# Cross attention: four places instead of three for the high and low halves of the probabilities

## The reference, cut to what matters

```
qh = (q @ wq.T)  -> 16 heads of 64          q = layernorm(x)
kh = (k @ wk.T), vh = (v @ wv.T)            k = v = ctx_1024
scores = einsum('bhqd,bhkd->bhqk', qh, kh) / sqrt(64)
attn   = softmax(scores, axis=-1)
ctx    = einsum('bhqk,bhkd->bhqd', attn, vh)
x      = x + ctx @ wo.T
```

## Time and profile before

| what | value |
|---|---|
| median of three runs | 3653.69 us |
| lowest, highest | 3648.0, 3655.38 us |
| span of the profiled execution | 3648.2 us |
| busy: TensorE, VectorE, ScalarE, GpSimd | 85%, 74%, 65%, 29% |
| mean granted TensorE clock | 0.937 |
| cross attention, about | 1853 to 3440 us |

### The profile page before, as it was taken

One profiled execution on the slowest core, in us unless ns is written; L12 is line 12 of the kernel. 1 busy time (PEld: TensorE's weight loads), 2 busy tenths in 40 slices (PEclk: granted clock), 3 DMA queues, 4 the chain that ended last, 5 costly groups with the idle time before them and its releaser, 6 DMA issues. The chain is left out here.

```text
span 3648.2 us, 78625 instructions
## 1 busy us (share of the span) xinstructions
PE 3088.9 (85%) x31124; PEld 1836.6 (50%) x31124; DVE 2698.1 (74%) x4017; ACT 2360.0 (65%) x4397; POOL 1058.4 (29%) x1854
## 2 busy tenths in 40 slices
PE   6999999978999755899778888998899879998824
PEld 3747474645665543444345554555455545555411
DVE  4748483867897765444469988889888988889688
ACT  3838373766786534333368887778777887788534
POOL 2232323156446234233212222222222222222122
PEclk9999999989999977999999999999999999999956
DMA  4050505175365376344399999999999999999843
GB/s 151 28 146 29 172 5 146 37 249 149 122 201 165 94 251 208 81 119 127 92 220 190 190 199 199 199 202 186 214 196 200 189 214 194 199 201 184 158 158 124
DMA packets 1309823, 582.40 MB, mean 160 GB/s; under 512 B 1144338, under 2 KB 1230994, under 8 KB 1306900
## 3 DMA queue, kind: packets, MB, share of 16 engines
q1 hardware_dynamic: 1305428, 560.60, 69.3%
q0 software_dynamic: 4032, 16.78, 1.2%
HBM read 183.63 MB, written 109.45 MB: 80 GB/s over the span
## 5 line engine op out<-in xcount | busy, mean ns | idle before, releaser
L2296 DVE SCALAR_TENSOR_TENSOR ca_halves<-ca_probs,ca_inv,ca_halves 128x1024 f16<-128x1024 f32 x512 | 655.5, 1280 | 109.9 <-ACT ca_halves L2222 102.4
L2288 DVE TENSOR_REDUCE ca_neg_max<-banks 128x1 f32<-128x1024 f32 x512 | 623.8, 1219 | 64.1 <-PE banks L2066 62.6
L2222 ACT ACTIVATE ca_halves<-ca_probs,ca_inv 128x1024 f16<-128x1024 f32 x512 | 586.6, 1146 | 102.9 <-DMA ca_pt<-ca_halves 99.1
L2214 ACT ACTIVATE ca_probs<-banks,ca_neg_max 128x1024 f32<-128x1024 f32 x512 | 568.7, 1111 | 72.6 <-DVE ca_neg_max L2288 70.7
L2032 POOL TENSOR_SCALAR ca_inv<-ca_total 128x1 f32<-128x1 f32 x512 | 97.5, 190 | 1197.1 <-ACT ca_probs L2214 1197.1
L2066 PE MATMUL banks<-ca_kt,ca_qt 64*128 64x512 f16 x3072 | 381.3, 382 | 48.8 <-ACT ca_probs L2214 47.1
L2088 PE MATMUL banks<-ca_pt,ca_v 128*64 128x256 f16 x6144 | 388.6, 277 | 0.9 <-DMA ca_pt<-ca_halves 0.8
L2088 PEld LDWEIGHTS banks<-ca_pt,ca_v 128*64 128x64 f16 x6144 | 318.6, 111 | 94.2 <-issue 78.4
L2035 POOL TENSOR_TENSOR ca_inv<-ca_inv,ca_minus_one 128x1 f32<-128x1 f32 x512 | 280.3, 548 | 42.6
L2066 PEld LDWEIGHTS banks<-ca_kt,ca_qt 64*128 64x128 f16 x3072 | 132.6, 95 | 238.8 <-issue 95.0
L2047 PE MATMUL banks<-ca_ct,ca_w 128*128 128x512 f16 x768 | 180.5, 386 | 48.1 <-DMA ca_ct<-ctx_part 23.8
(11 more groups left out here) (306 smaller groups left out, 5738.7 us busy)
## 6 DMA issues: line engine op xcount, KB each, us to landing
ca_w<-ca_w_parts SPq DMA_DIRECT2D x32, 768.0 KB, 5.4
wa_v<-v_rows SPq DMA_DIRECT2D x44, 264.0 KB, 4.5
v_rows<-wa_v_stage SPq DMA_DIRECT2D x32, 264.0 KB, 2.2
wa_x<-in_x SPq DMA_DIRECT2D x32, 256.0 KB, 5.3
wa_ring<-in_x SPq DMA_DIRECT2D x32, 256.0 KB, 3.9
x_after_window_attention<-wa_ring SPq DMA_DIRECT2D x32, 256.0 KB, 3.1
ba_tokens<-wa_tok_turned SPq DMA_DIRECT2D x32, 256.0 KB, 3.6
ba_xt<-ba_tokens SPq DMA_DIRECT2D x32, 256.0 KB, 7.2
```

What stands on the lines that cost most here:

```text
L2214: act.activation(probs[:, slot, :], scores(i), ACT.Exp, bias=neg_max[:, slot:slot + 1], accum_out=total[:, slot:slot + 1]).then_inc(exped, 1)
L2222: act.activation(halves[:, slot, 0, :], probs[:, slot, :], ACT.Copy, scale=inv[:, slot:slot + 1]).then_inc(split_hi, 1)
L2288: dve.tensor_reduce(out=neg_max[:, slot:slot + 1], in_=scores(i), axis=X_AXIS, op=ALU.max, negate=True).then_inc(maxed, 1)
L2296: dve.scalar_tensor_tensor(out=halves[:, slot, 1, :], in0=probs[:, slot, :], scalar=inv[:, slot:slot + 1], in1=halves[:, slot, 0, :], op0= ...
```

## The change

The ring `halves` gets 4 places (HALF_SLOTS) while `probs`, the scores and the row sums keep 3 (SLOTS). With it the number of `turned` semaphores goes from 3 to 4, and all that writes or reads `halves` indexes by i % 4. The high half of unit i now waits for the transpose of unit i - 4, and the low half for TensorE's turn of unit i - 4. TensorE waits for all four units of a group by name, since no two share a semaphore any more.

```
+HALF_SLOTS = 4
-        halves = sb("ca_halves", [P, SLOTS, 2, S], F16)
+        halves = sb("ca_halves", [P, HALF_SLOTS, 2, S], F16)
-        turned = [sem(f"ca_turned{i}") for i in range(SLOTS)]
+        turned = [sem(f"ca_turned{i}") for i in range(HALF_SLOTS)]
         def turned_by(i):
-            return 16 * (i // SLOTS + 1)
+            return 16 * (i // HALF_SLOTS + 1)
 (transpose, SyncE)
-                  halves[:, i % SLOTS, 0:parts, :].rearrange("p q s -> p (q s)")
-                  ).then_inc(turned[i % SLOTS], 16)
+                  halves[:, i % HALF_SLOTS, 0:parts, :].rearrange("p q s -> p (q s)")
+                  ).then_inc(turned[i % HALF_SLOTS], 16)
 (weigh, TensorE)
-                        for i in range(4 * g + 1, 4 * g + 4):
-                            pe.wait_ge(turned[i % SLOTS], turned_by(i))
+                        for i in range(4 * g, 4 * g + 4):
+                            pe.wait_ge(turned[i % HALF_SLOTS], turned_by(i))
 (high_half, ScalarE)
-                    if i >= SLOTS:
-                        act.wait_ge(turned[slot], turned_by(i - SLOTS))
-                    act.activation(halves[:, slot, 0, :], probs[:, slot, :], ACT.Copy,
+                    if i >= HALF_SLOTS:
+                        act.wait_ge(turned[i % HALF_SLOTS], turned_by(i - HALF_SLOTS))
+                    act.activation(halves[:, i % HALF_SLOTS, 0, :], probs[:, slot, :], ACT.Copy,
 (low_half, VectorE)
-                    if i - SLOTS in flipped_units:
-                        dve.wait_ge(low_flipped, flips_until(i - SLOTS))
+                    if i - HALF_SLOTS in flipped_units:
+                        dve.wait_ge(low_flipped, flips_until(i - HALF_SLOTS))
```

More of the change, by code:

```diff
@@ L2122, in flip_low @@
                         last = pe.transpose(bank[:, kb * P:(kb + 1) * P],
-                                            halves[:, i % SLOTS, 1, kb * P:(kb + 1) * P], consts.ident_h[:, :])
+                                            halves[:, i % HALF_SLOTS, 1, kb * P:(kb + 1) * P], consts.ident_h[:, :])
                     last.then_inc(low_flipped, 1)
@@ L2293, in low_half @@
                     dve.wait_ge(split_hi, i + 1)
-                    if i - SLOTS in flipped_units:
-                        dve.wait_ge(low_flipped, flips_until(i - SLOTS))
-                    dve.scalar_tensor_tensor(out=halves[:, slot, 1, :], in0=probs[:, slot, :],
-                                             scalar=inv[:, slot:slot + 1], in1=halves[:, slot, 0, :],
+                    if i - HALF_SLOTS in flipped_units:
+                        dve.wait_ge(low_flipped, flips_until(i - HALF_SLOTS))
+                    dve.scalar_tensor_tensor(out=halves[:, i % HALF_SLOTS, 1, :], in0=probs[:, slot, :],
+                                             scalar=inv[:, slot:slot + 1], in1=halves[:, i % HALF_SLOTS, 0, :],
                                              op0=ALU.mult, op1=ALU.subtract).then_inc(split_lo, 1)
```

## The result

The changed kernel takes 3621.51 us (median of four runs, 3621.0 to 3630.17) against 3654.53 us, a ratio of 0.9916 with an interval of 0.9901 to 0.9931. The forecast was 3620. Each ratio here is against the kernel before as it ran beside the changed one. Run once more with five rounds beside the last experiments it gave 0.9909 (0.9895 to 0.9923).

What follows compares the result with a forecast made beforehand. No single bound: TensorE fills tile turns, VectorE is nearest in ordinary turns, the queue's bursts delay sequence ends. Gains of 14.2 + 3 + 16.4 = 33.6 us off 3653.7 give 3620, range 3602 to 3645.

Steps and rivals of the forecast that it cites:

- Ordinary turns: The 11 turns without output projection, VectorE nearest to full: 14.2 us gained, bounds 8.9 and 19.5.
- Tile turns: The 12 turns with output projection, bound by TensorE, which hides nearly all the wait: 3 us gained, bounds 0 and 4.3.
- Sequence ends: The last two turns before each new sequence, three stretches: 16.4 us gained together, bounds 0 and 39.8.
- burst part: ScalarE and VectorE leave each 4 MB burst of loads one unit further ahead: 2.9 us a burst, 8.7 in all.
- all wait outside the bursts: At sequence ends, ScalarE's 15.5 us of wait not in the bursts: half taken as gain, 7.7 us.
- its wait stays under 5 us: Expected in the changed profile: TensorE's wait for transposes, 0.8 us before, stays under 5 us.
- idle time before L2088: Sign that the prediction is wrong: idle time appearing before this source line; no size given.
- rival C: TensorE stalls at groups' first halves in tile turns and time grows: 3690, or 3645 at one third the price; chance 0.04.
- rival B: Only the jitter goes: bursts gain nothing, ordinary turns only come down to 46.0; 13.2 us, 3640; chance 0.16.
- The added wait on TensorE: A group's first half waits for four semaphores instead of three: taken at 0, upper bound 9 us.
- The sum: 14.2 + 3 + 16.4 = 33.6 us, taken unscaled off the median of 3653.7 to give 3620.
- Rival A: The DMA queue is the bound, so the wait moves and the time stays: 3651 (3646 to 3655); chance 0.12.

Runs made afterwards that it cites:

- the last experiments: Changed kernel with burst loads reordered: tokens two each at steps 52 and 53, one each at 56 to 59, 3623.6 us; context in four 512 KB loads, 3628.28 us.
- the next place: Changed kernel with five places instead of four, the output projection using one half of its weights twice to make room: 3618.98 us, ratio 0.9921.
- the sixth place: Changed kernel with six places instead of four, the same half of the output weights left out as with five: 3623.09 us in a single run.

## Why the prediction was right, step by step

- **Ordinary turns**, forecast 14.2 us (8.9 to 19.5): 17.5. The middle was too low. The quickest turn before, 46.0, was no floor; it still held 0.8 us of ScalarE's wait. At 45.2 VectorE is busy for 214.57 of 226.1 us, and of its idle time 6.3 us end with a high half of ScalarE and 4.3 with scores of TensorE. That the 6.3 come from ScalarE's copies for turns made on TensorE is argued; the fastest turn without such copies, 44.1, where VectorE no longer waits for a high half, fits it.
- **Tile turns**, forecast 3 us (0 to 4.3): 3.8. They come to 51.0 or 51.1, the length that was read as TensorE's bound. ScalarE's wait in them was 38.6 us before, so TensorE hid nine tenths of it. (In the changed kernel the queue also carries 16 stores of results and 15 loads of the residual, 256 KB each, between 2580 and 3230 us, which the list of transfers in "The kernel before" does not name; the rates in the earlier trace rows hold them.)
- **Sequence ends**, forecast 16.4 us: 12.7. This term was mis-sized, above all in its burst part. The burst turns, the second of each pair, fell from 166.4 to 160.5 us: 2.0 a burst where 2.9, one whole unit, was forecast; the next place gave 2.2. So a further place does count in a burst, but less than a unit. The first turns of the pairs fell from 144.4 to 137.6, by 6.8 (forecast for all wait outside the bursts: 7.7), which is more than the 6.1 us that ScalarE waited in them. What was not counted is that TensorE then meets the same late transposes: 5.5, 4.4 and 6.2 us in the three bursts, 16.1 in all, where the prediction said that its wait stays under 5 us and named idle time before L2088 as a sign of being wrong. That sign came, in the bursts alone. It is rival C's mechanism in rival B's place. The burst turns still came out shorter, so ScalarE's gain was the larger there; how much of the missing 0.9 us a burst is TensorE's wait was not measured. The stretches come to 99.2 to 99.6 us, just above the 98 to 99 forecast.
- **The added wait on TensorE**, forecast 0: 0. With it and the old wait of ScalarE the time is that of before, within the interval.
- **The sum**: 33.6 forecast, 34.6 in the sublayer (0.7 of it in the first turn, which I had left out), 33.0 between the medians. Two terms too low and one too high cancel: that the total came within 2 us is partly luck, while the three gains lie in the turns and at the engines that the prediction named.
- **Rival A**, the queue as the bound, was false for ordinary turns, but by a small margin, as the kernel without TensorE's turns shows. The prediction's 41.7 of 46.0 us counted 16 whole units, though two in each of these turns have their low half turned by TensorE and send half; and it took rates of 205 to 241 GB/s, where the full queue gave 203. The two errors offset each other in part: a twentieth of the turn was spare, not a tenth. The Trainium skill's 261 GB/s (page "DMA: Bandwidth & Descriptors", section "Latency and other measured facts") would by estimate have left the kernel without TensorE's turns room, since 16 units then take 32 of 45.7 us and leave 14 for the weights; the trace does not agree, as it shows a full queue at 203. The page gives that figure for one form of transpose, and no run here shows whether these are of it.
- **Rival C** said that TensorE loses time in the tile turns. It has no wait for transposes there at all.

What stays open: why the sixth place gives less than the fifth (293.8 against 291.6 us, single profiles), what holds the odd first turn of the kernel without weights' loads, and whether TensorE's wait in a burst could be moved behind its scores, which was not tried.

## What to carry to other kernels

A wait that is short, frequent and passed on from engine to engine is worth nearly its whole sum where the last engine in line is the nearest to being full (here 17.5 of 19.5 us in ordinary turns), and almost nothing where another one is the bound (3.8 of 38.6 in tile turns): read the gain turn by turn, each against the engine that fills it, before adding up. One more place in a ring removes the unevenness of a queue that has room on average; a backlog by sheer bytes it shortens by less than a unit (2.0 of 2.9 us) and hands on, for the rest, to the next engine in line. When a ring is made longer, look for the in-order engine that waits for the same event.

## What the runs showed of the hardware

In the bursts TensorE works at half its clock for some us. In the changed kernel, in the first burst (timeline of TensorE, then two windows of it), the 24 matmuls behind the wait of 5.51 us take 2.77 us, and the same 24 take 1.50 a little later:

```profile
2190.91 2.77 PE L2089 MATMUL banks<-ca_pt,ca_v 128*64 128x256 f16 x24 [5.51 <-DMA ca_pt<-ca_halves]
2193.62 1.81 PE L2067 MATMUL banks<-ca_kt,ca_qt 64*128 64x512 f16 x12
2195.36 1.50 PE L2089 MATMUL banks<-ca_pt,ca_v 128*64 128x256 f16 x24
...
2190.91:2193.62 2.71, 2.71 (x25) 2.30 (x26) 2.62 (x3) 2.71 (x4) 0.74 (x2) 0.50 1.63 227
2195.36:2196.79 1.43, 1.43 (x26) 1.23 (x25) 1.32 (x2) 1.15 (x1) 0.00 (x0) 1.00 1.22 274
```

The granted clock is 0.50 in the first group and 1.00 in the second, the levels of 1.2 and 2.4 GHz. So the wait of 5.51 us cost another 1.6 here: 1.27 in the group and 0.3 in the scores behind it, which take 1.5 elsewhere. I had not priced that when I weighed rival C. It is no fixed price: behind the third burst's wait of 6.18 us the group is slow (2.77) and the scores are not (1.52), and in the second burst the scores before the wait of 4.45 us are slow as well (2.74, behind 2.96 us of waiting for ScalarE). Nor is it new with the change. In the kernel before, the scores at 2189.16 took 2.74 us at a granted clock of 0.50, behind 2.69 us of waiting for ScalarE, and the granted clock of the sequence ends shown was 0.95 and 0.97, against 0.97 and 0.97 now. The Trainium skill's page "TensorE: Matmul & The Clock Gate" (section "Part 1: The HAM clock gate") says that an array that has been idle runs at 1.2 GHz, half its full clock; the trace agrees, with 0.50 behind the 5.51 us.

The DMA queue, with packets under way nearly all the time, moved 203 GB/s of transposes and weights' loads (five ordinary turns without TensorE's turns), and 230 to 233 GB/s in the turns with a burst.
